# An audio encoder with self-attention on one core: attend of one key tile split over two periods, query halves on two columns of arrays

## What is computed

```
x = waveform.reshape(B, T // 80, 80)                    # 1500 tokens of 80 samples
h = einsum('bfr,hr->bfh', x, W) + b                     # to 256 channels
h = gelu(layernorm(h) * ln_gamma + ln_beta)
...
Q, K, V = projections of layernorm(h), 16 heads of 16   # S = 1500
attn = softmax(Q K^T / 4);  out = attn V
h = h + out @ Wo.T + bo
...
h = h + layernorm(layernorm(h) (+ routed attention)) * ln_g + ln_b
```

## Time and profile before

| | |
|---|---|
| median of three runs | 2262.24 us |
| profiled execution | 2263.96 us, span 2261.9 us |
| granted TensorE clock, mean | 0.984 |
| ACT busy | 2129.2 us, 94% |
| PE busy | 2076.9 us, 92% |
| DVE, POOL busy | 971.5 us (43%), 390.4 us (17%) |
| first and last exponential | about 82 and 2230 us |

### The profile page before, as it was taken

The page is one execution under the profiler, slowest core; times in us unless marked ns, Lnnn a source line. Parts: engine busy times, 40 slices in busy tenths (PEclk is TensorE's granted clock), DMA queues, the critical chain, the costliest instruction groups (busy, mean ns, idle before and its releaser), DMA issues.

```text
span 2261.9 us, 122306 instructions
## 1 busy us (share of the span) xinstructions
PE 2076.9 (92%) x56576; PEld 877.0 (39%) x56576; DVE 971.5 (43%) x2291; ACT 2129.2 (94%) x2346; POOL 390.4 (17%) x637
## 2 busy tenths in 40 slices
PE   4898999999999999999999899999999999999886
PEld 2433444344433444334443344334443434433223
DVE  6344244452545434463345524454254542433115
ACT  2599999999999999999999999999999999999994
POOL 2212011130112201131021301222011220111003
PEclk7999999999999999999999999999999999999998
DMA  2312121221112221221121212122111121122001
GB/s 72 87 35 55 45 57 42 59 55 46 47 50 56 58 52 41 56 63 52 46 52 38 72 49 53 44 57 55 46 48 50 51 55 46 38 63 56 19 10 37
DMA packets 115895, 113.84 MB, mean 50 GB/s; under 512 B 41666, under 2 KB 111861, under 8 KB 115376
## 3 DMA queue, kind: packets, MB, share of 16 engines
q1 hardware_dynamic: 111560, 103.08, 17.9%
q10 hardware_dynamic: 3816, 2.85, 0.6%
HBM read 55.16 MB, written 36.86 MB: 41 GB/s over the span
## 4 chain that ended last, share of the span: by engine, by line
ACT 67%; PE 16%; issue 6%; DVE 3%; POOL 3%; DMA 2%; SPq 2%; POOLq 1%; DVEq 1%; ACTq 0%
ACT prob L595 67%; PE PS L1080 7%; PE PS L1050 4%; PE PS L972 2%; PE PS L1002 1%; DMA oT<-Osb 1%; PE PS L952 1%; SPq L342 1%; SPq L306 1%; POOL rs L439 1%; PE PS L987 1%; PE PS L1027 1%; POOL Y L468 1%; DMA thin<-Osb 0%; POOL Hs L453 0%
## 5 line engine op out<-in xcount | busy, mean ns | idle before, releaser
L595 ACT ACTIVATE prob<-PS 125x1000 f32<-125x1000 f32 x2304 | 2077.2, 1087 | 49.2 <-PE PS L1050 46.9
L1080 PE MATMUL PS<-prob,Vst 64*17 64x500 f32 (+1 forms) x18432 | 1209.1, 580 | 1.8 <-DVE Hs L761 0.6
L1050 PE MATMUL PS<-QA,KA 64*32 64x500 f16 (+1 forms) x18432 | 951.2, 378 | 104.5 <-ACT prob L595 94.0
L1050 PEld LDWEIGHTS PS<-QA,KA 64*32 64x32 f16 (+1 forms) x18432 | 266.9, 90 | 1066.6 <-ACT prob L595 1040.4
L1080 PEld LDWEIGHTS PS<-prob,Vst 64*17 64x17 f32 (+1 forms) x18432 | 338.2, 93 | 47.8 <-issue 19.1
L461 POOL TENSOR_TENSOR sq<-HL 128x500 bf16<-128x500 f16 x96 | 97.9, 1020 | 950.0 <-DVE HL L694 950.0
L692 DVE TENSOR_SCALAR HL<-PS,b_qk 128x500 f16<-128x500 f32 x90 | 66.5, 739 | 435.5 <-PE PS L972 435.5
L972 PE MATMUL PS<-zT,w_qk 64*32 64x250 f32 x5760 | 235.5, 381 | 16.3 <-DVE Osb L744 13.5
L468 POOL TENSOR_TENSOR Y<-Hs,be_ln 125x256 f32<-125x256 f32 x96 | 70.2, 732 | 470.1 <-DVE Hs L761 470.1
L1002 PE MATMUL PS<-w_o,oT 64*32 64x128 f32 (+1 forms) x6144 | 128.4, 273 | 11.7 <-DMA oT<-Osb 8.8
L972 PEld LDWEIGHTS PS<-zT,w_qk 64*32 64x32 f32 x5760 | 104.1, 107 | 81.7 <-DVE Osb L744 24.5
(11 more groups left out here) (88 smaller groups left out, 941.4 us busy)
## 6 DMA issues: line engine op xcount, KB each, us to landing
qk_halves_scratch<-HL SPq DMA_DIRECT2D x96, 250.0 KB, 2.3
QA<-qk_halves_scratch SPq DMA_DIRECT2D x384, 62.5 KB
KA<-qk_halves_scratch SPq DMA_DIRECT2D x368, 62.5 KB
oT<-Osb SPq DMA_DIRECT2D x384, 31.2 KB, 2.2
out<-Y SPq DMA_DIRECT2D x23, 448.0 KB
X<-in_x SPq DMA_DIRECT2D x16, 234.4 KB
thin<-Osb SPq DMA_DIRECT2D x96, 7.8 KB
Den<-thin SPq DMA_DIRECT2D x96, 7.8 KB
```

Source lines behind the costliest of these rows:

```text
L595: act.activation(prob[0:T, 2 * (w % 6):2 * (w % 6) + 2, :], PS[0:T, 2 * (w % 2):2 * (w % 2) + 2, 0:QC], ACT.Exp, scale=scl)\
L1050: last = pe.matmul(PS[lo:hi, bank, 0:QC], KA[rows, G % NG, h // 2, t * T + lo:t * T + hi], QA[rows, G % NG, h // 2, c * QC:(c + 1) * QC], ...
L1080: last = pe.matmul(PS[lo:lo + HD + 1, bank + r, 0:QC], Vst[rows, b % 2, t, g * HG + j, :], prob[rows, (HG * t + j) % 12, :], start=(t == 0 ...
```

## The change

`attend` is now called with a period k: t = k // 2 is its key tile, p = k % 2 its pair. It takes the two heads of the pair that was exponentiated last, h = 0 and 1, and two halves q of the 500 queries: head h, half q on column j = 2h + q of the arrays, in 250 columns of the bank that begin at p * 250. It runs in every period from 2 on (twice in period 2, for pairs 0 and 1) and in period 0 for the last pair of the unit before. Pieces and their periods stay. A head's result now lies in two quadrants of partitions, so `store_attended` issues eight DMAs of 16 partitions by 250 queries instead of four by 500; the last unit's are split, four on SP and four on ACT. Counts of s_os double.

```
-            def attend(n, t):
-                b, g, bank = n // NU, (n % NU) // NC, 4 + 2 * (n % 2)
-                if t == 0:
+            def attend(n, k):
+                b, g, bank, t, p = n // NU, (n % NU) // NC, 4 + 2 * (n % 2), k // 2, k % 2
+                if k == 0:
                     pe.wait_ge(s_free, at(s_free, FREED[UNIT_USES[n]]))
                     if n > 1:
                         pe.wait_ge(s_ov, at(s_ov, n - 1))
                 for r, rows in halves(T):
-                    for j in range(HG):
-                        lo = 2 * HD * j
-                        last = pe.matmul(PS[lo:lo + HD + 1, bank + r, 0:QC], Vst[rows, b % 2, t, g * HG + j, :],
-                                         prob[rows, (HG * t + j) % 12, :], start=(t == 0), stop=(t == NT - 1))
-                last.then_inc(s_pv, 1)
+                    for j in range(4):
+                        h, q = j // 2, j % 2
+                        last = pe.matmul(PS[2 * HD * j:2 * HD * j + HD + 1, bank + r, p * QC // 2:(p + 1) * QC // 2],
+                                         Vst[rows, b % 2, t, g * HG + 2 * p + h, :],
+                                         prob[rows, 2 * (k % 6) + h, q * QC // 2:(q + 1) * QC // 2],
+                                         start=(k == 0), stop=(t == NT - 1), skip_group_check=True)
+                if p == 1:
+                    last.then_inc(s_pv, 1)
...
-                    if k % 2 == 0 and k:
-                        attend(n, k // 2 - 1)
+                    if k == 2:
+                        attend(n, 0)
+                    if k >= 2:
+                        attend(n, k - 1)
                     elif k == 0 and n > 0:
-                        attend(n - 1, NT - 1)
+                        attend(n - 1, WIN - 1)
                     beside(b, u, k)
...
+        def store_attended(eng, n, queries=(0, 1)):
...
+            for q in queries:
+                for j in range(HG):
+                    row, p = (g * HG + j) * HD, j // 2
+                    quadrant = 4 * HD * (j % 2) + 2 * HD * q
+                    eng.dma_start(oT[row % 128:row % 128 + HD, row // 128, oslot(b, c), q * QC // 2:(q + 1) * QC // 2],
+                                  Osb[quadrant:quadrant + HD, p * QC // 2:(p + 1) * QC // 2]).then_inc(s_os, 16)
...
-                store_attended(B * NU - 1)
+                store_attended(sp, B * NU - 1, (0,))
...
+                store_attended(act, B * NU - 1, (1,))
...
             def take_sums(n):
                 if n > 0:
-                    dve.wait_ge(s_os, at(s_os, 64 * n))
+                    dve.wait_ge(s_os, at(s_os, 128 * n))
...
```

More of the change, by code:

```diff
@@ L269, in audio_tower @@
             s_stp: sum(len(OFFSETS[key[0]]) - 1 for key, use in USE.items() if use >= FIRST or key[0] == "tok"),
[L270 removed]
+            s_ov: per_unit, s_pk: 16 * per_unit, s_rc: per_unit, s_up: 16 * per_unit, s_on: per_unit, s_os: 128 * per_unit,
             s_s1: per_tile, s_r3: per_tile, s_y: per_tile, s_yst[0]: STORED[0], s_yst[1]: STORED[1],
@@ L307, in lay_out @@
                       .then_inc(s_ld, 16)
+        def store_attended(eng, n, queries=(0, 1)):
+            b, u = n // NU, n % NU
+            g, c = u // NC, u % NC
+            eng.wait_ge(s_on, at(s_on, n + 1))
+            if g == 0 and b * NC + c > NC:
+                pb, pc = (b * NC + c - NC - 1) // NC, (c - 1) % NC
+                eng.wait_ge(s_full, at(s_full, USE["out", pb, CT * pc + CT - 1] + 1))
+            for q in queries:
[4 more added lines that the diff above has]
+                                  Osb[quadrant:quadrant + HD, p * QC // 2:(p + 1) * QC // 2]).then_inc(s_os, 16)
         ROWS = ((0, 112), (112, T))
@@ L331, in gather_sums @@
                 sp.dma_start(Den[0:128:2 * HD, :].rearrange("j (s c) -> j s c", s=25), thin[:, :]).then_inc(s_up, 16)
[L333 to L339, removed]
-                for j in range(HG):
-                    row = (g * HG + j) * HD
-                    sp.dma_start(oT[row % 128:row % 128 + HD, row // 128, oslot(b, c), :],
-                                 Osb[2 * HD * j:2 * HD * j + HD, :]).then_inc(s_os, 16)
             def store_out(b, c):
@@ L368, in run @@
                         if k == NORMALISE[u] and n > 0:
-                            store_attended(n - 1)
+                            store_attended(sp, n - 1)
                         if k == NORMALISE[u] + 1:
@@ L994, in output @@
                 if step == 0:
-                    pe.wait_ge(s_os, at(s_os, 64 * (b * NU + (NG - 1) * NC + e // CT + 1)))
+                    pe.wait_ge(s_os, at(s_os, 128 * (b * NU + (NG - 1) * NC + e // CT + 1)))
                 begin("out", b, e, step)
@@ L1191, in run @@
                 pe.wait_ge(s_free, at(s_free, FREED[LAST]))
-                attend(B * NU - 1, NT - 1)
+                attend(B * NU - 1, WIN - 1)
                 for e in range(CT + 1, NT):
```

## The result

The change made the kernel slower: 2494.57 us (median of four, 2488.36 to 2496.15) against 2261.45 us (median of four, 2260.44 to 2265.55). The ratio is 1.1022, 95% interval 1.0998 to 1.1046, so +233 us where +100 was forecast.

The account below looks back on a forecast made before the run. ACT's exponentials, fed with scores by PE, were taken as the bound. Turns 3, instructions 74, stores 27 and later pieces -4 gave +100 on a median of 2262.24 us: 2362 us, range 2280 to 2415.

Parts of the forecast that it names:

- The bound, and what feeds it: ACT, busy 94% with exponentials, bounds the kernel; PE feeds it scores; at most 47 us could be won back.
- Arithmetic of the attend: Attend on PE: same columns on the same arrays, 0.42 us per half attend, none gained or lost; cost 0.
- Turns: Periods with a turn's four transposes plus a half attend run some 0.13 us over the slack, 42 times: +3 us.
- Twice the attend instructions: PE's instruction stream: 36,864 more instructions, 144 more fetches, more fetch stalls in dense stretches: +74 us, bounds 0 to +120.
- a reserve of 212 instructions: PE has some 212 instructions left from an on-time fetch start; in output/value stretches that falls from 2.97 to 2.38 us.
- a stall gives the next fetch a head start, so two in three: Output/value stretches: of 216 fetches, 144 stall, at 0.5 us each: 72 us.
- They take the odds of today's output/value stretches: Query/key stretches: 9% of 208 fetches stall by 0.95 us: 18 us.
- Rule of the skill: The Trainium skill says the next 256-instruction block is fetched hidden; by it the fetch term is 0, the sum 2289 us.
- Rival B: Fetching becomes the bound: the 216 dense fetches take 3.5 us each instead of 2.87; 2427 us, chance 0.15.
- Eight stores: SP issues four more stores per unit, delaying unit 3 (13 us) and unit 4 (14 us): +27 us, bounds +5 to +38.
- +2.45 before the layouts behind them: SP's queue: four more store issues at 0.61 us delay the layouts behind them, and take_sums, by 2.45 us.
- Pieces start later: Pieces start 0.42 us later in their period, so those waiting for DVE wait less: -4 us.

Follow-up runs that it names:

- e2: The changed kernel with four stores of 16 by 500 per unit in place of eight, halves left unsorted in oT: 2424.97 us, 1.0730.
- e1: The kernel before with eight stores of 16 partitions by 250 queries per unit in place of four by 500, PE's program untouched: 2320.85 us, 1.0247.
- e4: The kernel before with eight one-column bf16 matmuls added per period, 36,864 more PE instructions with next to no array time: 2435.30 us, 1.0774.
- e7: The kernel before with eight one-column matmuls per period only beside no output, value or query/key step, 13,424 instructions added: 2268.63 us, 1.0036.
- e6: The kernel before with eight one-column matmuls per period only beside output and value steps, 10,832 instructions added: 2340.05 us, 1.0341.
- e9: The kernel before with all four stores per unit issued by GpSimd and the load of x moved behind the inverses' return: 2271.87 us, 1.0046.
- e11: The changed kernel with exponentials and values in bf16, so each attend matmul is one pass, eight stores kept: 2314.47 us, 1.0243.
- e12: The kernel before with exponentials and values in bf16, attend matmuls in one pass: 2250.81 us, 0.9962.

## Why the prediction was wrong, and where it was right

- **The bound, and what feeds it: right.** ACT's exponentials kept their pace, and they start late for want of scores: 173 of the 233 us are plain waits, and most of the rest is hidden in records that overlap less.
- **Arithmetic of the attend, cost 0: right.** Scores, half attend, next scores in unit 5 of the changed kernel, 0.42 us from the second to the third:

```profile
826.53 0.41 PE L1055 MATMUL PS<-QA,KA 64*32 64x500 f16 x8
...
826.76 0.61 PE L1087 MATMUL PS<-prob,Vst 64*17 64x250 f32 x16
827.18 0.40 PE L1055 MATMUL PS<-QA,KA 64*32 64x500 f16 x8
```

- **Turns, +3: small, as forecast.** With four stores (e2) the periods at turns cost 0.2 us more than before. The 12 us that they lose in e1 are unit 5's, from the stores.
- **Twice the attend instructions, +74: the mechanism right, the size wrong.** e2 gives 163, e4 173. The step that failed is the pricing of each late fetch by itself: an on-time start with a reserve of 212 instructions, a chance of a stall, and then "a stall gives the next fetch a head start, so two in three". The reserve from an on-time start is about right. But the next fetch is held back until some 2.6 us after the landing, so block starts are 3.3 us apart at least and 3.9 in the median. What is late stays late until a thin stretch lets it recover, and the reserve is spent once, not at each block. By stretch, e2 against before: beside output and value steps 80 us, where 72 less today's part was forecast; that is near, but from two values that were taken and not read (0.4 of lateness, two in three), so in part by luck. Beside query/key steps it is 35 where 18 was forecast; beside empty periods and the other pieces 37 where nothing was. At 128 instructions per 1.79 us, a block in 3.6 us, query/key stretches stand at the ceiling themselves. "They take the odds of today's output/value stretches" was the second fault: today's stand among thin neighbours, these among dense ones. (The program has 412 odd periods with query/key and token steps, not 416, which changes nothing.)
- **Rule of the skill.** The Trainium skill (Runtime: NRT & Kernel Launch, section Instruction fetch mechanics) has the next block fetched unseen behind the current one. The traces agree with its block of 256 and with a fetch that runs while PE works. They contradict it on the fetch being hidden: 330 stops in the changed kernel, and 173 us for pads that do no work.
- **Rival B was the right picture,** with 0.15 against 0.60 for the forecast. Its evidence against, "3.5 is what today's densest program asks for", was no evidence: a stretch can ask for exactly the ceiling and show little. Its 2427 misses in two ways that partly cancel. In the output and value stretches it has 136 us where e2 lost 80: some 3.24 us for each of the 216 blocks in place of 3.5, so these stretches leave part of their lateness to those behind them. To all the rest it charged 18 us less today's 16, where e2 lost 72, and 27 to the stores, where 58 to 70 were measured.
- **Eight stores, +27: right in place, incomplete.** Issue is 0.61 to 0.74 us a store however short it is. Unit 3 was to lose 13 and lost 12 to 14 in e1; unit 4 was to lose 14 and lost 20. In the changed kernel these are the two places, to be held against the earlier trace rows:

```profile
761.95 0.10 PEld L1016 LDWEIGHTS PS<-sq,head_sel 128*32 128x32 bf16 x2 [2.90 <-DVE Osb L749]
...
780.45 5.92 SPq L321 DMA_DIRECT2D oT<-Osb  x8
...
787.60 0.68 DVE L747 COPY Osb<-PS 128x500 f32<-128x500 f32 x1 [3.68 <-DMA oT<-Osb]
```

  norm_sums waits 2.90 where 2.2 was forecast, the copy 3.68 where it was 1.73 before. The missing part is unit 5's 15 us, and in e1 another 4 in the tail. This is the second step that failed: the prediction counted "+2.45 before the layouts behind them" and priced nothing behind those; the next thing on SP's queue that someone waits for is the spread of the sums, in the next unit.
- **Pieces start later, -4: not seen.** In e2 there is no kind of piece beside which the periods are shorter in sum than before.
- **The total.** The stores alone (e1, 58) and the instructions alone (e4, 173) add up to 231 of the 233 measured, so the two losses hardly meet.

## What to carry to other kernels

Count TensorE's instructions, weight loads and both passes of fp32 included, per microsecond and stretch by stretch, and hold them against the distance at which the trace's fetches follow each other when pressed, here 256 per 3.3 to 3.9 us. A split into twice as many half-size matmuls is free for the array and is not free above that rate; well below it, it nearly is (0.6 us per 1000 instructions in e7). For an added DMA issue, follow the queue to the next transfer that anyone waits for, even when it belongs to the next round of the loop.

## What the runs showed of the hardware

- The last fetches of a program left out, a fetch of TensorE's instructions starts 2.17 us or more after the one before has landed, in every trace, even while TensorE stands still; in the changed kernel it is 2.6 to 2.7 in the median where TensorE is ahead. After a stop PE resumes some 1.36 us after the landing.
- One-column pads cost 0.6 us per 1000 in thin stretches, 7.4 in dense ones (e7, e6).
- GpSimd pauses by up to 2.5 us, 44 us in 57 cases at one line, when it issues DMAs among its other work (e9; none over 0.2 us at that line before).
- With fewer passes in the attends, PE 73 to 75% busy instead of 92%, the mean granted clock was 0.927 (e11) and 0.941 (e12) instead of 0.984, and e12 was the fastest all the same.
